# Router products strewn over attention's last steps, and 16 unread products ahead of the first expert block

## The reference, cut to what matters

```python
x = x + jnp.tanh(g_xattn[0]) * _L0_xattn_ref(_layernorm(x, axis=-1), ctx_1024, ctx_1024, ...)
x = x + jnp.tanh(g_ffn[0]) * _L0_ffn_ref(_layernorm(x, axis=-1), ...)
x = x + jnp.tanh(g_xattn[1]) * _L1_xattn_ref(_layernorm(x, axis=-1), ctx_1024, ctx_1024, ...)
x = x + jnp.tanh(g_ffn[1]) * _L1_ffn_ref(_layernorm(x, axis=-1), ...)
# _L1_ffn_ref
logits = x @ W_router
expert_idx = jnp.argmax(logits, axis=-1)
h = jax.nn.gelu(jnp.einsum('th,ehi->tei', x, W1) + b1, approximate=False)
intermediate = jnp.einsum('te,tei->ti', onehot, h)
y = _layer_norm(intermediate @ Wo + bo + x, ln_gamma, ln_beta)
```

## Time and profile before

| what | value |
|---|---|
| device time, median of 3 runs | 830.56 us (826.97 to 832.3) |
| the profiled execution | 835.91 us, of which the span of instructions 834.1 us |
| busy in the span | PE 737.3 us (88%), DVE 581.4 (70%), ACT 440.8 (53%), POOL 296.2 (36%) |
| granted clock of TensorE, mean of the span | 0.925 of full |
| chain that ended last, by engine | PE 56%, issue 11%, DVE 11%, DMA 8%, POOL 6% |

### The profile page before, as it was taken

One profiled execution on the slowest core, in us unless ns is written; L12 is line 12 of the kernel. 1 busy time (PEld: TensorE's weight loads), 2 busy tenths in 40 slices (PEclk: granted clock), 3 DMA queues, 4 the chain that ended last, 5 costly groups with the idle time before them and its releaser, 6 DMA issues.

```text
span 834.1 us, 12041 instructions
## 1 busy us (share of the span) xinstructions
PE 737.3 (88%) x4096; PEld 428.6 (51%) x4096; DVE 581.4 (70%) x1126; ACT 440.8 (53%) x840; POOL 296.2 (36%) x348
## 2 busy tenths in 40 slices
PE   5897599999998998999768999899999886899991
PEld 3443234343432676777523334333353775799981
DVE  5473689999970489265758899799943537577775
ACT  2222488888887535665016888687853422233330
POOL 2121255555554234755000000755423304233322
PEclk9897699999999999999877999999975989899996
DMA  8497355454444431002722255522012202111100
GB/s 298 112 180 219 108 179 180 169 170 155 166 166 155 152 101 51 1 1 73 173 62 81 71 175 169 149 77 64 18 46 83 92 1 90 39 48 44 42 15 21
DMA packets 51357, 87.52 MB, mean 105 GB/s; under 512 B 8598, under 2 KB 16792, under 8 KB 51297
## 3 DMA queue, kind: packets, MB, share of 16 engines
q1 hardware_dynamic: 44320, 72.06, 28.2%
q0 software_dynamic: 4576, 11.54, 5.3%
q10 hardware_dynamic: 2400, 3.15, 1.1%
HBM read 45.29 MB, written 41.63 MB: 104 GB/s over the span
## 4 chain that ended last, share of the span: by engine, by line
PE 56%; issue 11%; DVE 11%; DMA 8%; POOL 6%; SPq 4%; ACT 3%; POOLq 0%; DVEq 0%; ACTq 0%
PE ps_out L712 14%; PE ps_a L698 10%; PE ps_wide L593 6%; DVE row_max L1395 5%; PE ps_misc L698 5%; PE ps_a L522 4%; DMA out_x<-sorted_rows,ids 3%; PE ps_a L830 3%; SPq L438 2%; PE ps_wide L688 2%; POOL sorted_rows L1287 2%; PE ps_wide L894 1%; POOL hid_lo L1255 1%; PE ps_out L844 1%; ACT probs L1020 1%
## 5 line engine op out<-in xcount | busy, mean ns | idle before, releaser
L1395 DVE TENSOR_REDUCE row_max<-ps_wide 128x2 f32<-128x1024 f32 x256 | 301.1, 1219 | 34.0 <-PE ps_wide L593 27.8
L1020 ACT ACTIVATE probs<-ps_a 128x512 f32<-128x512 f32 x342 | 191.5, 602 | 57.4 <-PE ps_a L698 49.4
L593 PE MATMUL ps_wide<-stack_k,stack_q 48*128 48x512 f32 x512 | 155.1, 472 | 15.2 <-DVE row_max L1395 11.0
L698 PE MATMUL ps_a<-stack_q,stack_k 62*128 62x512 f32 (+1 forms) x342 | 142.3, 467 | 13.1 <-ACT probs L1020 10.1
L712 PE MATMUL ps_out<-probs,vals 128*17 128x512 f32 x1024 | 142.2, 631 | 0.5 <-POOL probs L1214 0.5
L698 PEld LDWEIGHTS ps_a<-stack_q,stack_k 62*128 62x128 f32 (+1 forms) x342 | 61.9, 194 | 102.4 <-ACT probs L1020 69.3
L1020 ACT ACTIVATE probs<-ps_misc 128x512 f32<-128x512 f32 x170 | 102.4, 603 | 19.4 <-PE ps_misc L698 15.5
L1214 POOL TENSOR_TENSOR probs<-probs,fixes_sb 128x512 f32<-128x512 f32 x64 | 82.2, 1284 | 82.5 <-ACT probs L1020 82.5
L593 PEld LDWEIGHTS ps_wide<-stack_k,stack_q 48*128 48x128 f32 x512 | 63.0, 191 | 50.5 <-DVE row_max L1395 20.2
L698 PE MATMUL ps_misc<-stack_q,stack_k 62*128 62x512 f32 (+1 forms) x170 | 78.8, 463 | 2.9 <-ACT probs L1020 2.9
L1199 POOL TENSOR_SCALAR max_neg<-row_max 128x16 f32<-128x16 f32 x32 | 9.2, 289 | 158.5 <-DVE row_max L1395 137.3
(11 more groups left out here) (214 smaller groups left out, 1326.7 us busy)
## 6 DMA issues: line engine op xcount, KB each, us to landing
rows_sorted<-blank SPq DMA_DIRECT2D x17, 1040.0 KB, 5.0
planes_k<-planes SPq DMA_DIRECT2D x32, 256.0 KB, 3.8
planes_q<-planes SPq DMA_DIRECT2D x32, 256.0 KB, 3.5
stack_q<-planes_q SPq DMA_DIRECT2D x64, 128.0 KB, 2.8
stack_k<-planes_k SPq DMA_DIRECT2D x64, 128.0 KB, 2.8
w_raw<-in_L_W SPq DMA_DIRECT2D x6, 1024.0 KB, 5.1
stack_q<-planes_q SPq DMA_DIRECT2D x64, 64.0 KB, 2.7
stack_k<-planes_k SPq DMA_DIRECT2D x64, 64.0 KB, 2.6
```

The lines of the kernel that those rows point to most:

```text
L593: mm(raw_slot(l, ("pair", g, p))[:, i * S:(i + 1) * S], stack_q[at, slot(g, c) + q * P:slot(g, c) + (q + 1) * P], stack_k[at, slot(g, c):s ...
L698: mm(score_slot(("tile", n))[:], stack_k[at, slot(g, c) + k * P:slot(g, c) + (k + 1) * P], stack_q[at, slot(g, c):slot(g, c) + S], start=T ...
L1020: do(probs[n % PROBS[l]][:, j, :], score_slot(("tile", n * HG + j))[:], ACT.Exp, scale=0.25).then_inc(exp_done, 1)
L1395: v.tensor_reduce(row_max[:, g % 2, :, p], raw_slot(l, ("pair", g, p))[:].rearrange("p (i k) -> p i k", i=2), AX, ALU.max).then_inc(sem(f" ...
```

## The change

1. PE's order. `route_logits` takes the row tiles that it computes. Batch 0's four tiles go to: ahead of `weigh` of (14, 2), behind it, the middle of (14, 3), ahead of its `weigh`. Batch 1's transposes go behind `weigh` of (14, 3). Count 0 goes to the middle of (15, 0). Batch 1's four tiles go ahead of and behind `weigh` of (15, 0), to the middle of (15, 1), and ahead of its `weigh`. Count 1 and the total go behind `weigh` of (15, 2).
2. The order in which the two wide PSUM tensors are used (`raw_items`) follows.
3. ACT. The two copies of a batch's transposed rows stand one ahead of the first and one ahead of the second exponential of the step: of (14, 2) for batch 0, of (15, 0) for batch 1 (before: (14, 3)).
4. DVE. Three of batch 2's row updates go ahead of routing batch 0, its last and the statistics ahead of routing batch 1, group 13's division ahead of placing batch 1. Scaling batch 2's rows goes from ahead of the last two groups' divisions to behind them.
5. PE, ahead of block 0. Behind batch 2's router products and ahead of turning block 0's rows stand 16 products of 128x512 into the first wide PSUM tensor. Nothing reads them. The wait for the split weights moves ahead of them.

```diff
-                    for what, b in (("n3", 0), ("n3", 1), ("logits", 0), ("count", 0), ("logits", 1), ("count", 1)):
+                    for what, b in (("n3", 0), ("logits", 0), ("n3", 1), ("count", 0), ("logits", 1)):
                         yield (what, b)
+                if l == 1 and g == G + 2:
+                    yield ("count", 1)
...
-            def route_logits(b):
-
-                slot_free("logits", b)
-                if b == 0:
-                    pe.wait_ge(sem("w_last"), 16 * 7)
-                pe.wait_ge(sem("x3_ready"), C * (b + 1))
-                for q in range(QT):
+            def route_logits(b, qs=range(QT)):
+
+                if qs[0] == 0:
+                    slot_free("logits", b)
+                    if b == 0:
+                        pe.wait_ge(sem("w_last"), 16 * 7)
+                    pe.wait_ge(sem("x3_ready"), C * (b + 1))
+                for q in qs:
...
-                last.then_inc(sem("logits_done"), 1)
+                if qs[-1] == QT - 1:
+                    last.then_inc(sem("logits_done"), 1)
...
-                            if l == 1 and (g, k, c) == (G - 2, 2, 0):
-                                turn_n3(1)
+                            if l == 1 and (g, k, c) == (G - 2, 3, 0):
+                                route_logits(0, (2,))
+                            if l == 1 and (g, k, c) == (G - 1, 0, 0):
+                                count(0)
+                            if l == 1 and (g, k, c) == (G - 1, 1, 0):
+                                route_logits(1, (2,))
                         if l == 1 and (g, k) == (G - 2, 2):
-                            route_logits(0)
+                            route_logits(0, (0,))
                         if l == 1 and (g, k) == (G - 2, 3):
-                            count(0)
-                            route_logits(1)
+                            route_logits(0, (3,))
+                        if l == 1 and (g, k) == (G - 1, 0):
+                            route_logits(1, (0,))
+                        if l == 1 and (g, k) == (G - 1, 1):
+                            route_logits(1, (3,))
                         weigh(g * QT + k - BEHIND)
+                        if l == 1 and (g, k) == (G - 2, 2):
+                            route_logits(0, (1,))
+                        if l == 1 and (g, k) == (G - 2, 3):
+                            turn_n3(1)
                         if l == 1 and (g, k) == (G - 1, 0):
+                            route_logits(1, (1,))
+                        if l == 1 and (g, k) == (G - 1, 2):
                             count(1)
                             total(0)
...
             route_logits(2)
+            pe.wait_ge(sem("w1_low"), E * 4 + 2)
+            for _ in range(16):
+                mm(pw[0][:, 0:S], w1_hi[:, 0, 0:P], w1_hi[:, 0, 0:S], start=True, stop=True)
             turn_rows(0)
-            pe.wait_ge(sem("w1_low"), E * 4 + 2)
...
-                            if l == 1 and j == 0 and g == G - 2 and k - 2 in range(EARLY_ROWS):
-                                if k == 2:
-                                    act.wait_ge(sem("b1_split"), 1)
-                                rows1(k - 2)
+                            if l == 1 and (g, k, j) == (G - 2, 2, 0):
+                                act.wait_ge(sem("b1_split"), 1)
+                            if l == 1 and (g, k) == (G - 2, 2) and j < C:
+                                rows1(0, (j,))
+                            if l == 1 and (g, k) == (G - 1, 0) and j < C:
+                                rows1(1, (j,))
...
                     normalise(G - 4)
+                    for t in tiles(2, None)[0:3]:
+                        update3(t)
                     route(0)
                     place(0)
-                    for t in tiles(2, None)[0:2]:
-                        update3(t)
+                    update3(tiles(2, None)[3])
+                    aggregate(3, 2, 1e-5)
                     route(1)
+                    normalise(G - 3)
                     place(1)
-                    for t in tiles(2, None)[2:4]:
-                        update3(t)
-                    normalise(G - 3)
-                    aggregate(3, 2, 1e-5)
                     tables(0)
-                    normal(3, 2, x)
                     normalise(G - 2)
                     normalise(G - 1)
+                    normal(3, 2, x)
```

More of the change, by code:

```diff
@@ L987, in turned_out, with rows1 @@
                     do(xT[:, c, b * S:(b + 1) * S], spare_banks[c][:] if name == "n0" else wide(u), ACT.Copy).then_inc(sem(f"turned_read_{name}"), 1)
-            def rows1(b):
-                wait(act, sem("logits_done"), b)
-                for c in range(C):
+            def rows1(b, cs=range(C)):
+                if cs[0] == 0:
+                    wait(act, sem("logits_done"), b)
+                for c in cs:
                     act.wait_ge(sem("turned_n3"), b * C + c + 1)
```

## The result

The changed kernel took 842.27 us, median of 4 runs (834.46 to 844.53), beside 830.2 of the kernel before: ratio 1.0117, 95% interval 1.0072 to 1.0162 (it is not the quotient of the two medians, which is 1.0145). The median of all 16 runs is 840.6, that is 7.1 us or 0.85% over the 833.5 that the kernel before had in the later comparisons (35 runs, 826.0 to 841.4). The prediction was 836.0, or +5.4 us. The ratios and their intervals leave out the few runs that lie over 1.5% above the fastest of their kernel (three of scaling_alone's twelve, one of them at 920.16 us), the medians do not.

A forecast was written before the change was run, and what follows sets the result against it. PE at half clock was taken to bound attention's end, and PE's path the stretch behind it. Terms -0.5 + 2.2 + 3.7 = +5.4 us on the 830.56 median made 836.0, range 821 to 841 (the forecast's own 833 to 839).

The forecast's parts named there:

- The strewing, -0.5: Attention's end on PE: spreading router tiles between steps gives -0.9 to +1.0 us with an unchanged clock; taken as -0.5.
- The same two clocks: Attention's end: if the clock falls where it fell before, PE does the same work at unchanged full and half clock.
- Batch 1's late count, 0: Batch 1's count and scatters come later, but gather 0 stays hidden with 4 us to spare: costs nothing.
- ready before: POOL's root behind batch 1's scatters, at about 645.5, comes early enough to add nothing to batch 2's scaling.
- Scaling behind the divisions, +2.2: DVE scales batch 2's rows after the last division, and batch 2's transposes wait for it: +2.2 us on the path.
- rival S: Half clock reaches through batch 2's transposes, router passes and all 16 products: +9.6 us, 840.2; chance 0.18.
- second term: Batch 2's rows scaled behind the last division, making PE wait ahead of batch 2's transposes: +2.2 us.
- The 16 products, 5.3 less 1.6: Unread products ahead of block 0 cost 5.3 us on PE and give back 1.6 in block 0: +3.7 us.
- half and half: Of the 16 unread products, 8 run at half clock (3.4 us) and 8 at full (1.9 us).
- H: The clock holds at full through attention's end: -7.7 us, 822.9; chance 0.19.
- M: The clock falls later, in batch 1's strewn pairs, giving back 4 us: +1.4 us, 832.0; chance 0.15.
- N: The 16 products lie hidden in a wait for gather 0: about 0, 830.5 us; chance 0.05.

The follow-up runs named there:

- scaling_alone: Kernel before, with only batch 2's scaling moved behind the last two groups' divisions on DVE: 837.59 us, ratio 1.0040.
- after_again: The changed kernel run again without an edit: 840.03 us, median of 12, ratio 1.0086 to the kernel before.
- only_products: Kernel before plus the 16 unread products at the same place, nothing strewn: 837.34 us, ratio 1.0028.
- no_products: Changed kernel without the 16 unread products: 837.94 us, ratio 1.0059 to the kernel before.
- gap_products: Changed kernel with the 16 unread products moved ahead of batch 2's transposes, where PE idles: 836.05 us, ratio 1.0027 to the kernel before.
- scaling_back: Changed kernel with batch 2's scaling ahead of the last two divisions again: 839.21 us, ratio 1.0072 to the kernel before.
- filled: Kernel before plus 24 unread products in attention's last eight steps, ahead of score pairs and router row tiles: 835.01 us, ratio 1.0035.
- gap_ahead: Changed kernel with 8 unread products, ahead of batch 2's transposes, and scaling ahead of the last two divisions: 834.68 us, ratio 1.0016 to the kernel before.

## Why the prediction was right or wrong

In class it held, narrowly: +0.85% over all runs is within 1%, where it put 0.65; the first four runs alone were over. Their 842.27 lies 1.3 us above the upper end of the range, the 840.03 of after_again 1 us below it. The size, +5.4 against +7.1, is within what after_again's ratio allows (+3.9 to +10.5) and just under what the first four runs' does (+6.0 to +13.5). That the number came out near is no proof of the sum: one term was left out of it, one stood at nothing that has a price when alone, and one may have been too small a gain.

- **The strewing, -0.5.** Up to attention's end the gain was probably larger, but its size is not shown. Nine profiles with strewn tiles have 39.4 to 43.6 us there, mean 42.2; of the three without them or filling, before had 45.1, only_products 44.8, scaling_alone 42.4, mean 44.1. "The same two clocks" was wrong: the fall came 11.5 to 14.7 us behind the last maxima, as before (14.6), but in each of them the clock came back within 3.4 to 6.9 us, and fell again (in scaling_alone, without strewing, it came back too, after 23.8 us). As a part by itself the strewing nevertheless cost +3.0 (0.6 to 5.3). The timeline shows 2.4 of it behind attention, from the next step; with the shorter rest of attention its rows make only +0.7, so the remainder is not explained.
- **Batch 1's late count, 0.** The reasoning on gather 0 held, with room to spare. It asked who waits for the scatters' data and not what else stands behind them on POOL: batch 2's root. The prediction did look at the root and said "ready before", which is right only because the scaling was moved to behind the divisions. There it is hidden (no wait at 641.49 in the changed kernel); with the scaling ahead it is 1.1 us of PE's idle time. So, by the timelines, the late scaling covers the late root; the totals (8.6 for the parts, 7.2 to 9.7 for the whole) are too coarse to show it.
- **Scaling behind the divisions, +2.2.** The place and the size were right: PE's idle time about 3 us, ended by DVE's scaling, in both profiles and in scaling_alone; the way to batch 2's transposes is 2.1 to 2.4 longer.
- **What was left out of the sum: batch 2's router products at half clock, +1.6.** It is rival S, at 0.18, and it is what happened, in both profiles (3.43 for 1.81), in no_products and in scaling_alone. S's other half, slower transposes, happened only in scaling_alone (1.94 against 1.06). The forecast took before's clock at this place although its own second term put 2.2 us of idle time in front of it. That was the step that failed. Whether the idle time itself brings the fall or only moves the router products behind it is not settled; the rows under gap_products speak for the second.
- **The 16 products, 5.3 less 1.6.** 5.10 and 6.57 in the two profiles, 6.02 in scaling_back. The first profile is nearly the forecast's "half and half"; the 6.57, and the 6.48 of only_products, are nearer S's 6.9. What block 0 gives back was right, 1.6.
- **The rivals.** H is out in attention: the clock fell in every version, the filled one too. M is out as it was put: the clock fell no later than before; that it came back for a while may have given a part of the 4 us that M looked for. N is out: no wait of PE for gather 0, and the products cost their time. S's sum was 840.2, the changed kernel 840.6 over 16 runs. That agreement is partly luck: the kernel before had 830.56 in the prediction and 833.5 in the later comparisons, so S's step is +9.6 and the measured one +7.1, and S has transposes at +1, which did not come in the changed kernel.

By the rule that the prediction quoted from the Trainium skill ("TensorE: Matmul & The Clock Gate", "Why this matters for your kernels"), drops come from idle gaps between bursts. The rows agree with it in part behind attention: 3 us of idle time, then 0.50, and a later fall when the gap was filled (650.4 in gap_products, 669.3 in gap_ahead); but there was a fall at about the same place with 0.81 us of idle time too. They do not bear it out inside attention, where filled fell to 0.50 behind 18.9 us of 18.9 busy. The prediction used the second to set the rule aside everywhere.

What stays open: why the clock falls in attention's end with PE busy nearly throughout, what share of the fall behind attention the idle time has, and why one kernel's fall and return differ between executions (the changed kernel: 17.1 us at half in attention in one, 27.3 in the other).

## What to carry to other kernels

When an edit makes work later near a place where the clock falls, price that work at half clock too; here that was 1.6 us on top of 2.2 for the router products. Unread products pay only in time that PE would otherwise wait: 16 of them cost 2 to 5 us net behind the router and nearly nothing ahead of the transposes. When a result is made later, look at everything that stands behind its consumers in their queues, and test the parts alone as well as together, since one part can hide another's price.

## What the runs showed of the hardware that was not expected

- The granted clock fell from 1.00 to 0.50 with PE busy for 18.90 of 18.90 us (filled, by the records of its matmuls), and stayed there for 20.5 us of which PE was busy for all.
- It moved between its two levels, 2.4 and 1.2 GHz, eight times in 38 us (changed kernel, 614.6 to 652.2). There a router pair took 1.01 us at half clock against 0.61; the 16 products took 6.57 in after_again against 3.74 at full clock in gap_products.
- Identical instructions up to the last maxima took from 598.2 to 607.5 us. A single profile of a kernel like this one says where time goes, not how much: the changed kernel's first profile was faster than the one of before.
